# Residual with tokens on partitions, norms on GpSimd, spread rows and key copies by DMA: a four-layer transformer kernel

## The reference, cut to what matters

```
block 0:  nx = LN(x)*gamma + beta;  one-head attention of nx over the context
          combined = [nx, evidence, cond];  softmax router over 3 experts; 3 SiLU experts; sigmoid gate
          x = x + gate * (routed @ out_w + out_b)
block 1, 2 (16 heads of 8):
          shift_a, scale_a, gate_a, shift_m, scale_m, gate_m = split(silu(cond) @ W + b, 6)
          x = x + gate_a * proj(attn(LN(x)*(1+scale_a) + shift_a))
          x = x + cproj(attn(q of LN(x), k and v of the context))      # block 1: key mask; block 2: LN(context)
          x = x + gate_m * (gelu((LN(x)*(1+scale_m) + shift_m) @ W1 + b1) @ W2 + b2)
block 3:  the same three parts, each norm modulated by its own 1+gamma, beta of cond, q and k rotated, no gates
```

## Time and profile before

| | |
|---|---|
| median of 3 runs | 2663.71 us (2660.18 to 2665.43) |
| the profiled execution | 2663.34 us, of which its span is 2661.5 us; granted clock 0.992 |
| PE / PEld busy | 2502.8 / 1913.5 us |
| DVE / ACT busy | 2207.7 / 1850.3 us |
| POOL busy | 0.2 us |
| chain that ended last | PE 66%, DVE 15%, ACT 12%, issue 3%, DMA 2% |
| DMA | 37.63 MB, 14 GB/s on the mean |

### The profile page before, as it was taken

The page is one execution under the profiler, slowest core; times in us unless marked ns, Lnnn a source line. Parts: engine busy times, 40 slices in busy tenths (PEclk is TensorE's granted clock), DMA queues, the critical chain, the costliest instruction groups (busy, mean ns, idle before and its releaser), DMA issues.

```text
span 2661.5 us, 76369 instructions
## 1 busy us (share of the span) xinstructions
PE 2502.8 (94%) x32150; PEld 1913.5 (72%) x32150; DVE 2207.7 (83%) x3752; ACT 1850.3 (70%) x3862; POOL 0.2 (0%) x4
## 2 busy tenths in 40 slices
PE   4899999999999999999999999999999999999876
PEld 3766777777777777777777777777777777777654
DVE  3778878888888888888888888888888888888863
ACT  2576767777777777677777777777777777777653
POOL 0000000000000000000000000000000000000000
PEclk9999999999999999999999999999999999999997
DMA  6100000000000000000000000000000000000000
GB/s 129 35 8 2 8 13 14 10 12 14 14 14 8 10 12 14 14 14 14 8 10 12 14 14 14 8 10 12 14 14 14 14 4 10 8 10 10 4 3 5
DMA packets 57963, 37.63 MB, mean 14 GB/s; under 512 B 20192, under 2 KB 52768, under 8 KB 57632
## 3 DMA queue, kind: packets, MB, share of 16 engines
q1 hardware_dynamic: 49120, 32.72, 4.4%
q10 hardware_dynamic: 8512, 0.03, 0.2%
HBM read 28.44 MB, written 4.29 MB: 12 GB/s over the span
## 4 chain that ended last, share of the span: by engine, by line
PE 66%; DVE 15%; ACT 12%; issue 3%; DMA 2%; DVEq 0%
PE pair L583 15%; PE pair L591 14%; PE pair L628 11%; PE pair L644 6%; PE pair L613 6%; PE pair L649 5%; PE pair L657 4%; DVE mx L774 4%; DVE wide L776 4%; PE pair L598 2%; ACT vb L697 2%; ACT wide L1098 2%; ACT L667 2%; ACT L1098 1%; DMA km<-probs_by_expert 1%
## 5 line engine op out<-in xcount | busy, mean ns | idle before, releaser
L704 ACT ACTIVATE wide<-pair 128x1024 f32<-128x1024 f32 x384 | 392.2, 1023 | 172.8 <-PE pair L628 170.2
L774 DVE TENSOR_REDUCE mx<-pair 128x16 f32<-128x1024 f32 x320 | 389.5, 1217 | 86.6 <-PE pair L613 82.6
L628 PE MATMUL pair<-konst,wide 128*128 128x128 f32 x3072 | 407.2, 276 | 37.2 <-DVE wide L776 28.6
L628 PEld LDWEIGHTS pair<-konst,wide 128*128 128x128 f32 x3072 | 349.0, 142 | 109.5 <-DVE wide L776 64.0
L776 DVE TENSOR_TENSOR wide<-pair,mx 128x1024 f32<-128x1024 f32 x320 | 391.8, 1224 | 11.0
L683 ACT ACTIVATE wide<-pair,konst 128x256 f32<-128x256 f32 x352 | 165.9, 471 | 132.9 <-PE pair L583 132.6
L697 ACT ACTIVATE vb<-pair 64x128 f32<-64x128 f32 x768 | 208.5, 272 | 41.9 <-PE pair L598 25.5
L644 PEld LDWEIGHTS pair<-wide,vb 128*32 128x32 f32 x12288 | 181.6, 110 | 66.5 <-issue 24.0
L613 PE MATMUL pair<-km,qT 32*64 32x256 f32 x6144 | 218.5, 390 | 11.1 <-DVE qT L745 4.3
L583 PE MATMUL pair<-wide,konst 128*128 128x256 f32 x704 | 218.5, 399 | 5.1 <-ACT wide L677 4.5
L644 PE MATMUL pair<-wide,vb 128*32 128x64 f32 x12288 | 212.4, 221 | 8.7 <-ACT wide L704 6.8
(11 more groups left out here) (223 smaller groups left out, 4527.3 us busy)
## 6 DMA issues: line engine op xcount, KB each, us to landing
km<-probs_by_expert SPq DMA_DIRECT2D x32, 384.0 KB, 3.5
rows<-in_x_dram SPq DMA_DIRECT2D x32, 128.0 KB, 2.1
rows<-in_ctx_dram SPq DMA_DIRECT2D x32, 128.0 KB, 2.3
out_dram<-wide SPq DMA_DIRECT2D x32, 128.0 KB, 1.8
w0e<-in_L_xcond_e_w_dram SPq DMA_DIRECT2D x4, 384.0 KB, 5.5
w1fc<-in_L_xcond_fc_w_dram SPq DMA_DIRECT2D x2, 256.0 KB, 5.3
w2fc<-in_L_xcond_W_mlp_dram SPq DMA_DIRECT2D x2, 256.0 KB, 6.2
wide<-in_L_xcond_ffn_w_dram SPq DMA_DIRECT2D x2, 256.0 KB, 5.4
```

Of the source, the lines that this page charges most:

```text
L628: ins = pe.transpose(b[:, t:t + 128], G.ss[:, 2 * c + rr, a:a + 128], ident)
L704: act.activation(G.pT[:, :, 4 * c:4 * c + 4, :].rearrange("k p h q -> k p (h q)"), two_banks(name)[:].rearrange("k (p n) -> k p n", p=2), ...
L774: dve.tensor_reduce(top, heads(s), AX_X, ALU.max).then_inc(*tick("dve", ("max", G.n, tag, c)))
```

## The change

Only one launch and the same outputs; what moves is where the data stand and who computes.

- The residual x stands with tokens on partitions (`[128, TT, D]`, two tiles of 128 tokens), two buffers for each stream. It is loaded and stored by DMA as it is; only the context is still turned on the way in. Block 0's result is turned back once (`bk0`).
- A norm is: `bn_stats` and `bn_aggr` on VectorE; Ln and Exp on ScalarE over 128x2 values; on GpSimd (x - mean)*rstd, one instruction for each 128 tokens, and for the seven modulated norms a multiplication and an addition over 128x256; two turns on TensorE; one copy on ScalarE (which applies block 0's gamma and beta).
- The modulation and gate rows are computed in the setup as rows (`mods`, 128 x 22 x 128) and written to DRAM. Eleven sets a visit (`SETS`) are loaded by two DMAs each, every row spread over the 64 partitions of its sequence, into two slots for each stream.
- Projections and the second MLP product have the activations as the stationary side and give tokens on partitions. Output biases, or gate times bias, are added to x by GpSimd ahead of time.
- Key weights have their columns reordered, so that the rows of every fourth head are every fourth partition. `km` is zeroed once; the masked copies are four DMAs of 32 partitions each, out of `G.kT`. In blocks 1 and 2 ScalarE writes `kT` with the bias.
- GpSimd gets a queue in the planner; `ORDER`, `LEAD` and some costs are new.

```diff
-        def norm(G, tag, before, ready, scale, shift, dst, eps, src):
-            cen, var = (tag, "cen"), (tag, "var")
-            put_product(G, "cen" + tag, cen, PE_MM, [(center, src[:])], before, wait=[ready])
-            put(G, "sq" + tag, "act", ACT_256, lambda act: act_square(act, G, tag), "cen" + tag)
-            put_product(G, "var" + tag, var, PE_MM, [(average, squares(G, tag)[0])], "sq" + tag, wait=[("sq", G.n, tag)])
...
+        def norm(G, tag, before, ready, scale, dst, eps):
...
+            put(G, "st" + tag, "dve", DVE_STATS, dve_first, *before)
+            put(G, "rstd" + tag, "act", 0.48, lambda act: act_rstd(act, G, tag, eps), "st" + tag, table=EXP_TABLE)
+            if scale:
+                load_mods(G, tag)
+            put(G, "ap" + tag, "pool", POOL_APPLY + (2 * POOL_ADD if scale else 0), lambda pool: pool_apply(pool, G, tag), "rstd" + tag,
+                *(["ld" + tag] if scale else []))
+            put(G, "nT" + tag, "pe", 2 * PE_TURN, lambda pe: pe_turn_norm(pe, G, tag), "ap" + tag, takes=[((tag, "n"), 1)])
+            put(G, "xn" + tag, "act", ACT_BIAS if tag == "0" else ACT_256, lambda act: act_normed(act, G, tag, dst), "nT" + tag, gives=[(tag, "n")])
...
+        def dve_stats(dve, G, tag):
+            x, stats, mv, _, _ = norm_of(G, tag)
+            for t in range(TT):
+                dve.bn_stats(stats[:, t, :], x[:, t, :]).then_inc(*tick("dve", ("stats", G.n, tag, t)))
+            for t in range(TT):
+                dve.wait_ge(*done("stats", G.n, tag, t))
+                dve.bn_aggr(mv[:, t, :], stats[:, t, :]).then_inc(*tick("dve", *([("var", G.n, tag)] if t else [])))
...
+        def pool_apply(pool, G, tag):
+            x, _, mv, rstd, out = norm_of(G, tag)
+            pool.wait_ge(*done("rstd", G.n, tag))
+            modulated = tag in SETS
+            for t in range(TT):
+                pool.tensor_scalar(out[:, t, :], x[:, t, :], mv[:, t, 0:1], rstd[:, t:t + 1], ALU.subtract, ALU.mult)\
+                    .then_inc(*tick("pool", *([("whitened" if modulated else "normed", G.n, tag)] if t else [])))
+            if modulated:
+                pool.wait_ge(*mod_loaded(G, tag))
+                pool.wait_ge(*done("whitened", G.n, tag))
+                pool.tensor_tensor(out, out, mod_slot(G, tag)[:, :, 0, :], ALU.mult).then_inc(*tick("pool", ("scaled", G.n, tag)))
+                pool.wait_ge(*done("scaled", G.n, tag))
+                pool.tensor_tensor(out, out, mod_slot(G, tag)[:, :, 1, :], ALU.add).then_inc(*tick("pool", ("normed", G.n, tag)))
...
+        def sp_mods(sp, G, tag):
+            n, k = loads(G, tag), SETS.index(tag)
+            if n > 2:
+                before, last = (G.n, SETS[k - 2]) if k >= 2 else (G.n - NS, SETS[k - 2])
+                if last[1] in "gh":
+                    end = last[0] + "s" if last[1] == "g" else last[0]
+                    sp.wait_ge(*done("gated", before, end))
+                    sp.wait_ge(*done("biased", before, end))
+                else:
+                    sp.wait_ge(*done("normed", before, last))
+            rows = mods_dram[G.n * GB:(G.n + 1) * GB, k, :].rearrange("(t b) n -> b t n", b=2)
+            for b2 in range(2):
+                sp.dma_start(mod_slot(G, tag)[64 * b2:64 * b2 + 64].rearrange("p t w d -> p t (w d)"),
+                             rows[b2:b2 + 1].broadcast_to((64, TT, 2 * D))).then_inc(mod_loaded(G, tag)[0], 16)
...
+            put(G, "ld" + tag, "sp", 0.15, lambda sp: sp_mods(sp, G, tag), *users, lag=2.3)
...
+        def sp_keys(sp, G, tag):
+            n = copies(G, tag)
+            if n > 1:
+                before, last = (G.n - NS, "3x") if tag == "1s" else (G.n, attentions[attentions.index(tag) - 1])
+                sp.wait_ge(*done("mm", (before, last, "s", 1)))
+            sp.wait_ge(*done("kT", G.n, tag))
+            for j in range(JH):
+                sp.dma_start(G.km[j:128:JH, j, :], G.kT[j:128:JH, :]).then_inc(keys_in[G.stream], 16)
...
+            put(G, "kT" + tag, *(("dve", 3 * DVE_256 + HOP) if L == 3 else ("act", ACT_BIAS)), kT, "k" + tag, *last[0:1], gives=[(tag, "k")])
+            put(G, "km" + tag, "sp", 0.3, lambda sp: sp_keys(sp, G, tag), "kT" + tag, *last[-1:], lag=2.2)
...
         def pe_scores(pe, G, tag):
             pe.wait_ge(*done("qT", G.n, tag))
-            pe.wait_ge(*done("km", G.n, tag))
+            pe.wait_ge(keys_in[G.stream], 16 * JH * copies(G, tag))
...
+        def pe_token_product(pe, name, pairs):
+            b = claim(pe, name)
+            for t in range(TT):
+                for i, (m, w) in enumerate(pairs):
+                    ins = pe.matmul(b[:, t * 128:(t + 1) * 128], m[:, t * 128:(t + 1) * 128], w, start=(i == 0), stop=(i == len(pairs) - 1))
...
+        def add_gated(G, name, tag, end, norm_tag, after):
+            load_mods(G, tag)
+            put(G, "b" + end, "pool", POOL_ADD, lambda pool: pool_gated_bias(pool, G, ("normed", G.n, norm_tag), tag, end), "ap" + norm_tag, "ld" + tag)
+            put(G, "gt" + end, "dve", DVE_PTR, lambda dve: dve_gated(dve, G, name, tag, end), after, "ld" + tag, gives=[name])
+            put(G, "x" + end, "dve", 0.43, lambda dve: dve_add_gated(dve, G, end), "gt" + end, "b" + end)
...
             def sp_store(sp):
-                sp.wait_ge(*done("rows", n))
+                sp.wait_ge(*done("x", n, "3"))
+                sp.dma_start(token_rows(out_rows, n), G.x[:]).then_inc(stored[G.stream], 16)
```

More of the change, by code:

```diff
@@ L177, in __init__ @@
     def __init__(self, pieces):
-        self.order = {e: [] for e in ("pe", "act", "dve", "sp")}
+        self.order = {e: [] for e in ("pe", "act", "dve", "pool", "sp")}
         self.where, self.before, self.begin = {}, {}, {}
@@ new lines, in pe_turn_norm, with act_normed @@
+        def pe_turn_norm(pe, G, tag):
+            pe.wait_ge(*done("normed", G.n, tag))
+            b = claim(pe, (G.n, tag, "n"))
+            out = norm_of(G, tag)[4]
+            for t in range(TT):
+                ins = pe.transpose(b[:, t * 128:(t + 1) * 128], out[:, t, :], ident)
+            ins.then_inc(*tick("pe", ("mm", (G.n, tag, "n"))))
+        def act_normed(act, G, tag, dst):
+            name = (G.n, tag, "n")
+            act.wait_ge(*done("mm", name))
+            if tag == "0":
+                act.activation(dst[:], tile(name)[:, 0:T], ACT.Identity, scale=col("L0_xcond_ln_gamma"), bias=col("L0_xcond_ln_beta"))\
+                    .then_inc(*tick("act", ("free", name), ("xn", G.n, tag)))
+            else:
+                act.activation(dst[:], tile(name)[:, 0:T], ACT.Copy).then_inc(*tick("act", ("free", name), ("xn", G.n, tag)))
@@ L802, in dve_norm0 @@
[L802 to L808 removed]
+            dve.wait_ge(*mod_loaded(G, tag))
@@ new lines, in dve_gated, with dve_add_gated @@
+            dve.tensor_tensor(change, tile(name)[:, 0:T].rearrange("p (t d) -> p t d", t=TT), mod_slot(G, tag)[:, :, 0, :], ALU.mult)\
+                .then_inc(*tick("dve", ("free", name), ("gated", G.n, end)))
+        def dve_add_gated(dve, G, end):
+            change = G.tmp[:, 3, :].rearrange("p (t d) -> p t d", t=TT)
+            dve.wait_ge(*done("biased", G.n, end))
+            dve.wait_ge(*done("gated", G.n, end))
+            dve.tensor_tensor(G.x[:], G.x[:], change, ALU.add).then_inc(*tick("dve", ("x", G.n, end)))
@@ L940, in dve_hidden0 @@
             name, (n, m, _) = (G.n, "0", "h", k), hidden_halves(G, k)
-            if k == 0 and G.n >= NS:
-                dve.wait_ge(stored[G.stream], 16 * (G.n // NS))
             dve.wait_ge(*done("mm", name))
@@ L1207, in put_visit @@
+                norm(G, m, ["x" + c], done("x", n, c), True, G.xn, eps)
+                b1 = {1: "fc1_b", 2: "b_mlp1", 3: "ffn_b1"}[L]
+                mlp(G, m, L, ACT.Gelu_apprx_tanh if L == 2 else ACT.Gelu, p + b1, gm, f"{L}")
                 if L == 1:
-                    norm(G, "2c", "mix" + c, ("c", n), None, None, G.cn, 1, G.cT)
-            def pe_out(pe):
-                pe.wait_ge(*done("x", n, "3"))
-                b = claim(pe, (n, "out"))
-                for t in range(TT):
-                    ins = pe.transpose(b[:, t * 128:(t + 1) * 128], G.x[:, t * 128:(t + 1) * 128], ident)
-                ins.then_inc(*tick("pe", ("mm", (n, "out"))))
@@ L1217, in put_visit @@
-            put(G, "out", "pe", 2 * PE_TURN, pe_out, "x3", takes=[(("out",), 1)])
-            put(G, "rows", "act", ACT_256, lambda act: act_out(act, G, ("out",), G.tmp[:, 0, :], 0.0, ("rows", n)), "out", gives=[("out",)])
-            put(G, "store", "sp", 0.1, sp_store, "rows", lag=2.0)
+                    norm(G, "2c", ["mix" + c], done("mm", (n, c, "o")), False, G.cn, 1)
+            put(G, "store", "sp", 0.1, sp_store, "x3", lag=2.0)
         for G in visits:
@@ L1246, in _ @@
                     piece.emit(act)
+            @block.gpsimd
+            def _(pool):
+                for piece in plan.order["pool"]:
+                    piece.emit(pool)
             @block.vector
@@ L1271 @@
```

(10 more changed lines are left out.)

376 lines of the change are left out of this document (210 added, 166 removed), and 75 rows, old and new, of the table ORDER.

## The result

| | median | lowest to highest |
|---|---|---|
| before, beside it | 2661.3 us | 2655.5 to 2668.6 (20 runs) |
| changed | 2679.6 us | 2660.4 to 2693.4 (20 runs) |

The ratio is 1.0063, 95% interval 1.0046 to 1.008: slower by 0.6%. The profiled execution of the changed kernel took 2663.2 us, near the lower end of its runs, with a span of 2661.4 us and a granted clock of 0.984.

What follows compares the result with a forecast made beforehand. TensorE's work was taken to set the 78.6 us period; 78.6 - 7.3 + 1.8 = 73.1 us, and 64.5 + 32 x 73.1 + 95 + 1.8 = 2500 us, range 2410 to 2665.

Steps and rivals of the forecast that it cites:

- Four streams still cover it: Visit length: alone some 210 us, against 4 x 73 = 292 in flight, so the longer norms and keys stay covered.
- SP's 1.8 us: Late self-attention keys from SP's DMAs: up to 4.5 us a visit, 40% of it taken, +1.8 us on the period.
- I take about twice VectorE's, 0.8 and 0.45: GpSimd instruction prices: 0.8 us for 128x256, 0.45 for 128x128; 27 us a visit, 2.5 in a modulated norm.
- so throughput costs nothing: GpSimd: its sum of 15 to 41 us a visit lies under the period, so only latency in the norm's chain counts.
- waits put down to a DMA: Sign of being right: TensorE idle before the scores, put down to a DMA, near 2 us a visit.
- The sign that I had named: TensorE's waits before norm turns, released by POOL, exceeding those before scores would mean GpSimd's latency, not SP, was mis-sized.
- the -7.3 forecast: TensorE's work: norms lose products and gain turns, in and out -0.2; -7.3 us a visit, the whole expected gain.
- VectorE and ScalarE: Busy time a visit after the change: VectorE 59 us (69 at the upper end), ScalarE 54, neither the bound.
- VectorE against GpSimd: Rival: two-SBUF-input VectorE instructions and GpSimd hold each other up, 2.5 us or +3; period 76 us, 2593 us; chance 0.18.
- Outside the visits: Setup, fill and drain: +10 us before the loop and +4 for fill and drain, 161.3 us in all beside the visits.
- The SP queue sets the period: Rival: 18 operands a visit through SP each cost TensorE 0.5 us, 9 us; period 80.3 us, 2731 us, slower; chance 0.13.
- the likeliest one: The forecast's own case: period 73.1 us, 2500 us; chance 0.42.

Runs made afterwards that it cites:

- e1: Changed kernel with one of the two GpSimd whitening instructions of each norm left out, same order: 2567.9 us, ratio 0.9644 to before.
- e14: Changed kernel's instructions, only GpSimd's whitening price corrected in the plan (1.6 for 0.8 us), order chosen anew: 2607.0 us, ratio 0.9773 to before.
- e2: Changed kernel with one key DMA for each attention in place of four, same order: 2606.3 us, ratio 0.9787 to before.
- e4: Changed kernel with half the whitening, one key DMA per attention and rows loaded only for each stream's first two sets: 2464.7 us, ratio 0.9255 to before.

## Why the prediction was wrong, point by point

**The step that failed is "Four streams still cover it"**, the latency of GpSimd's piece in the norms: the sum has no term for it, its only wait being SP's 1.8 us. It rests on a price that was mis-sized, "I take about twice VectorE's, 0.8 and 0.45". The additions at 0.75 lie near the 0.8 taken. The whitening is 0.81, not 0.45, above my upper bound (0.64) as well, so GpSimd's part of a modulated norm is 2 x 0.81 + 0.73 + 0.77 = 3.1 us, not 2.5. I set GpSimd's sum beside the period and found room, rightly on the mean (33 of 80 us a visit), but "so throughput costs nothing" left out that its work comes in bursts and queues. And a fixed order covers only what it was laid out for: the plan has 0.8 for a pair that takes 1.6, and TensorE met many norms' turns too early. The row to look at was the planner's cost beside my own bounds, as I did for SP and not for GpSimd. Cost: 162.8/32 = 5.1 us of idle a visit, for which the forecast had nothing; e1 shows it by a shorter piece, e14 by a right plan.

**SP.** The mechanism was right, its size too small. I took 0.51 us a DMA; key copies take 0.61 and row loads 0.65. Landing of a 32 KB copy, 1.8, lies within 1 to 3.5. I allowed 1.8 us a visit and found 2.3 ahead of the scores (74.3/32), not all of it SP's; by removal keys and rows are worth (74 + 47)/32 = 3.8. My sign for it, waits put down to a DMA, did not appear: the profile names whichever semaphore came last before (`ACT wide L1246`, `issue`), and only e2 showed whose wait it was.

**The sign that I had named shows it.** I wrote that if waits before a norm's turns, released by POOL, exceed those before scores, GpSimd's latency is what I mis-sized: 162.8 against 74.3.

**TensorE: right.** 77.1 us of busy time a visit before, 300.49/320 x 74.0 = 69.5 in e4: -7.6 for the -7.3 forecast. In the changed kernel it is 70.8, at a lower clock. The windows of e4:
```profile
1040.00:1360.00 320.00, 300.49 (x4350) 241.86 (x4334) 254.24 (x554) 236.39 (x528) 103.85 (x136) 1.00 0.05 16
```
**VectorE and ScalarE: right.** 59.2 and 54.7 us for 59 and 54; bn_stats 0.284 and bn_aggr 0.174 for 0.28 and 0.17.

**VectorE against GpSimd: acts, and is small.** Sums of two SBUF tiles took 0.425 before; L907 means 0.464 and L850 0.511, and the one at 1452.89 above took 0.97 beside L791. (0.039 x 128 + 0.086 x 64)/32 = 0.33 us a visit in these two groups. Over all 512 VectorE instructions that add, subtract or multiply two SBUF tiles, what each took above the shortest of its line and tiles sums to 27 us, 0.86 a visit, on an engine with 20 us to spare. GpSimd pays as well: L784 means 0.810 against a median of 0.796, L791 0.768 against 0.725, with single ones of 1.65 and 1.59; 0.6 us a visit, in the norm's chain. By the Trainium skill (SBUF — State Buffer, "Who interferes with whom") the two exclude each other; the trace agrees: the L907 at 1452.89 began 0.03 us behind L791, outlasted it by 0.28 us and took 0.97 in place of 0.43. As the main cause of this result it is out: e4 has as much of it on VectorE (26 us in all) and its visits take 74.0 us.

**Outside the visits.** I took 161 us; it is 2663.2 - 32 x 80.1 = 100, and 84 with the 80.6 of twenty visits. The loop starts at 62.6 us, 8 later than before where 10 were forecast, so fill and drain became shorter. The stores show how: before, the last four leave at 2493.7 to 2658.7 us, one visit behind the other; in the changed kernel at 2613.3 to 2658.5, so four visits end almost together. I didn't isolate why; `LEAD`, 39.5 before and 13.5 after, is the candidate. It is luck that this error hid 60 us or more of the other: the period alone, 80.1 for 73.1, would give 2724.

**The chances.** 0.13 for slower went to "The SP queue sets the period", at 80.3 us. The period came out there by coincidence, with GpSimd as the larger cause, and the time did not (2731). The range ended at 2665 because I left that case out of it, and let the uncertain deliveries shift the likeliest one by 1.8 us only.

## What to carry to other kernels

- Where the order on each engine is fixed from planned costs, a new operation's planned cost is a claim: set it beside the nearest rows of every engine that gets new work. One that is half the real length costs idle time at its reader, even on an engine that is 60% idle.
- "The engine has room" answers throughput. In a chain that a visit passes eleven times, also add up the length, and ask whether the order, not the number of streams, covers it, and whether the work comes in bursts: this GpSimd, 40% busy on the mean, is 93% busy in the 12 us shown below.
- Don't judge a change by an order made for other costs, nor mend the costs and keep the offsets (+6.7% here). Correct the costs, choose the order anew for both kernels, and compare these: here 1.006 became 0.959, good to a per cent or two, as two orders for the same costs differed by 1.9%.
